# DLRM tower on one core: two-operand one-hot compares, paired lookups, gathers in eights

## The reference

```python
e = stack([tbl_f[ids[:, f]] for f in range(26)], axis=1)      # 2048 x 26 x 128
combined = concatenate([e, r_dense_x[:, None, :]], axis=1)    # 2048 x 27 x 128
z = einsum('bfd,bgd->bfg', combined, combined)[:, TRIU_I, TRIU_J]   # 351 pairs
h = concatenate([z, r_dense_x], axis=1)                       # 2048 x 479
h = maximum(h @ W_top1 + b_top1, 0)                           # 512
h = maximum(h @ W_top2 + b_top2, 0)                           # 256
y = h @ W_top3                                                # 2048 x 1
```

## Time and profile before

| | |
|---|---|
| Time, median of 3 runs | 373.29 us (373.04 to 374.13) |
| Profiled execution | 374.87 us |
| Its span, first to last instruction | 373.1 us |
| TensorE matmuls busy | 339.7 us (91%) |
| Weight loads busy | 312.7 us (84%) |
| VectorE busy | 194.0 us (52%) |
| ScalarE busy | 184.3 us (49%) |
| GpSimd busy | 254.9 us (68%) |
| Mean granted TensorE clock | 0.995 of full speed |

### The profile page before, as it was taken

The page is one execution under the profiler, slowest core; times in us unless marked ns, Lnnn a source line. Parts: engine busy times, 40 slices in busy tenths (PEclk is TensorE's granted clock), DMA queues, the critical chain, the costliest instruction groups (busy, mean ns, idle before and its releaser), DMA issues.

```text
span 373.1 us, 13958 instructions
## 1 busy us (share of the span) xinstructions
PE 339.7 (91%) x6176; PEld 312.7 (84%) x6176; DVE 194.0 (52%) x700; ACT 184.3 (49%) x234; POOL 254.9 (68%) x265
## 2 busy tenths in 40 slices
PE   0775879599999999999999999999999999999986
PEld 0775879598989988999989989999888988998776
DVE  1998758274645734575645634575545635541020
ACT  3783711673337463573437552582526552574332
POOL 6877777777777777777777777776777677771000
PEclk9998999999999999999999999999999999999999
DMA  7974761221532216222432126221442122210000
GB/s 266 368 244 157 223 215 53 52 66 53 177 87 67 57 52 208 57 66 52 145 115 72 51 54 206 51 72 47 121 142 67 46 59 66 53 50 26 16 2 4
DMA packets 15777, 37.17 MB, mean 100 GB/s; under 512 B 5125, under 2 KB 7813, under 8 KB 15716
## 3 DMA queue, kind: packets, MB, share of 16 engines
q0 software_dynamic: 8192, 16.79, 16.8%
q1 hardware_dynamic: 7524, 19.48, 15.5%
HBM read 36.24 MB, written 0.01 MB: 97 GB/s over the span
## 4 chain that ended last, share of the span: by engine, by line
PE 86%; POOL 5%; issue 4%; ACT 3%; DMA 3%; ACTq 0%
PE ps_lk L442 38%; PE ps_gram L469 14%; PE ps_tr L454 8%; PE ps_mlp L499 8%; PE ps_zt L499 7%; POOL rows L218 5%; PE ps_mlp L508 4%; PE ps_zt L508 4%; DMA rows<-in_tbl,gather_ids 2%; PE ps_mlp L516 2%; PE ps_zt L486 2%; ACT xt L319 1%; ACT xt L309 1%; DMA gather_ids<-in_ids_gather 1%; ACT ids_from L304 0%
## 5 line engine op out<-in xcount | busy, mean ns | idle before, releaser
L218 POOL DMA_INDIRECT rows<-in_tbl,gather_ids x256 | 253.5, 990 | 82.3 <-issue 70.7
L252 DVE TENSOR_SCALAR onehot<-ids_from 128x256 fp32r<-128x256 f32 x640 | 151.7, 303 | 59.3 <-PE ps_lk L442 42.6
L442 PE MATMUL ps_lk<-onehot,table 128*128 128x256 f32 x1280 | 166.9, 289 | 13.2 <-DVE onehot L252 11.5
L442 PEld LDWEIGHTS ps_lk<-onehot,table 128*128 128x128 f32 x1280 | 159.1, 195 | 13.9 <-issue 12.4
L319 ACT COPY xt<-ps_tr 128x512 f32<-128x512 f32 x64 | 76.6, 1197 | 96.5 <-PE ps_tr L454 94.6
L260 DVE STREAM_TRANSPOSE zs<-ps_gram 128x832 f32<-128x832 f32 x16 | 16.8, 1050 | 91.9 <-PE ps_gram L469 91.9
L469 PEld LDWEIGHTS ps_gram<-xt 128*26 128x26 f32 x4096 | 43.5, 103 | 19.5 <-issue 16.0
L469 PE MATMUL ps_gram<-xt 128*26 128x26 f32 x4096 | 52.2, 192 | 5.5 <-issue 1.3
L309 ACT COPY xt<-ps_lk 128x512 f32<-128x512 f32 x40 | 48.6, 1226 | 13.4 <-PE ps_lk L442 7.9
L454 PE MATMUL ps_tr<-ident,rows 128*128 128x128 f32 x256 | 39.9, 278 | 9.2 <-ACT xt L319 4.5
L454 PEld LDWEIGHTS ps_tr<-ident,rows 128*128 128x128 f32 x256 | 29.8, 141 | 13.2 <-issue 5.3
(11 more groups left out here) (30 smaller groups left out, 102.4 us busy)
## 6 DMA issues: line engine op xcount, KB each, us to landing
ids<-in_ids_onehot SPq DMA_DIRECT2D x16, 640.0 KB, 5.2
rows<-in_tbl,gather_ids POOLq DMA_INDIRECT x256
w<-in_tbl SPq DMA_DIRECT2D x6, 512.0 KB, 5.8
h<-in_tbl SPq DMA_DIRECT2D x2, 512.0 KB, 5.9
zt<-in_tbl SPq DMA_DIRECT2D x2, 512.0 KB, 5.7
dense_x<-in_dense SPq DMA_DIRECT2D x8, 128.0 KB
zt<-in_dense SPq DMA_DIRECT2D x8, 128.0 KB, 2.4
w<-in_w SPq DMA_DIRECT2D x1, 512.0 KB
```

What stands on the lines that cost most here:

```text
L218: pool.indirect_dma_start(rows[n % ROW_BUFS][:, r, :], None, t_[f"tbl_{GATHERED[r]}"], bass.IndirectOffsetOnAxis(ap=gather_ids[:, n, r:r + ...
L252: nc.vector.tensor_scalar(onehot[:, u % RING, :], ids_from[:, j, :], float(k), None, ALU.is_equal).then_inc(s_unit, 1)
L442: m = nc.tensor.matmul(bank(c, i)[:, j % 2, :], table[:, j, part, k, :], onehot[:, u % RING, :], start=(k == 0 and part == 0), stop=(k == ...
```

## The change

The one-hot rows. A unit is now one k for both tables of a lookup (512 columns), so a chunk has 40 units and the ring holds 8. In chunk 0 one compare with a number makes a unit, after both tables' subtractions. In chunks 1 to 7 (`make_pairs`) one two-operand compare makes two units (1024 elements): the ids of two tables, repeated for two k, against `row`, a small tile with the numbers 0 to 7 in each partition, two of them repeated along the samples. POOL and VectorE make `row` at the start.

The lookups. Both tables of a lookup are done side by side: for each k, table a high and low, table b high and low. The number and the shape of the matmuls stay. The ids are loaded and shifted in parts of 4 and 6 tables instead of 5 and 5.

The gathers. They are issued in eights (half a tile). The wait for the turn of the group is gone; a half waits for a count of used units (LEAD, the first two tiles and one half) or of grams.

The order. In chunk 0 each lookup is followed by one turn, and the third tile's turns move into chunk 1's loop. `layer2(c - 1, 1)` and `gram(c, 1, 1)` of the last chunk come before its `turn_pairs`. The last MLP runs layer by layer over both tiles, with banks of its own from those that the lookups no longer need, and both halves of y are copied at once.

```diff
-RING = 16
-UNITS = NO * KT
+RING = 8
+UNITS = LP * KT
+USE = 2
+CUT = (0, 4, NO)
+LEAD = (0, 2, 6, 10, 16)
+LAST = (CHUNKS - 1) * MLP_USES
...
-        onehot = sb("onehot", [P, RING, CS], F32R)
+        onehot = sb("onehot", [P, RING, 2, CS], F32R)
+        row = sb("row", [P, KT])
...
+        def last1_bank(t, j):
+            return ps_lk[j][:, 0, 0:P] if j < LB else (ps_tr, ps_mlp)[t][:, 0:P]
+        def last2_bank(t, j):
+            return ((ps_tr, ps_zt)[j][:, 0:P], ps_lk[j][:, 0, 0:P])[t]
+        def last3_bank():
+            return ps_lk[2][:, 0, :]
...
         @block.gpsimd
             def gather(n, g):
-                if n >= ROW_BUFS:
-                    pool.wait_ge(s_tr, (n - ROW_BUFS) * NGR + g + 1)
-                    pool.sem_inc(s_carrier["pool"], 1)
                 for r in GROUPS[g]:
...
-            for n in range(ROW_BUFS):
-                for g in range(NGR):
-                    gather(n, g)
-            for n in range(ROW_BUFS, TILES):
+            for n in range(TILES):
                 for h in range(2):
-                    pool.wait_ge(s_gpart, (n - 2) * PARTS + h + 1)
+                    b = n * PARTS + h
+                    if 0 < b < len(LEAD):
+                        pool.wait_ge(s_unit_used, LEAD[b])
+                    elif b >= len(LEAD):
+                        pool.wait_ge(s_gpart, max(b - 2 * PARTS, 0) + 1)
                     gather(n, 2 * h)
                     gather(n, 2 * h + 1)
...
         @block.vector
-                    nc.vector.tensor_scalar(onehot[:, u % RING, :], ids_from[:, j, :],
+                    nc.vector.tensor_scalar(onehot[:, u % RING, :, :], ids_from[:, 2 * i:2 * i + 2, :],
                                             float(k), None, ALU.is_equal).then_inc(s_unit, 1)
+            def make_pairs(c, lo, hi):
+                for u in range(lo, hi, USE):
+                    i, k = divmod(u, KT)
+                    if k == 0 and 2 * i in CUT:
+                        dve.wait_ge(s_from, c * 2 + (CUT.index(2 * i) + 1))
+                    dve.wait_ge(s_unit_used, (c * UNITS + u - RING) // USE + 1)
+                    nc.vector.tensor_tensor(
+                        onehot[:, u % RING:u % RING + USE, :, :].rearrange("p u a s -> p u (a s)"),
+                        ids_from[:, 2 * i:2 * i + 2, :].rearrange("p a s -> p (a s)").unsqueeze(1).to_broadcast([P, USE, 2 * CS]),
+                        row[:, k:k + USE].unsqueeze(2).to_broadcast([P, USE, 2 * CS]), ALU.is_equal
+                    ).then_inc(s_unit, USE)
...
-                make_units(0, j * KT, (j + 1) * KT)
-            make_units(1, 0, 2 * PU)
+                if j % 2 == 1:
+                    make_units(0, (j - 1) // 2 * KT, (j + 1) // 2 * KT)
+            make_pairs(1, 0, 2 * KT)
...
         @block.tensor
-                for j in (2 * i, 2 * i + 1):
+                for k in range(KT):
+                    u = i * KT + k
                     if c == 0:
-                        pe.wait_ge(s_low, j + 1)
-                    for k in range(KT):
-                        u = j * KT + k
-                        if k % 2 == 0:
-                            pe.wait_ge(s_unit, c * UNITS + u + 2)
+                        pe.wait_ge(s_unit, u + 1)
+                    elif k % (KT // 2) == 0:
+                        pe.wait_ge(s_unit, c * UNITS + u + KT // 2)
+                    for j in range(2):
                         for part in range(2):
-                            m = nc.tensor.matmul(bank(c, i)[:, j % 2, :], table[:, j, part, k, :],
-                                                 onehot[:, u % RING, :],
+                            m = nc.tensor.matmul(bank(c, i)[:, j, :], table[:, 2 * i + j, part, k, :],
+                                                 onehot[:, u % RING, j, :], start=(k == 0 and j == 0 and part == 0),
...
-            lookup(0, 0)
-            turn(0, 0, 0)
-            lookup(0, 1)
-            turn(0, 0, 1)
-            turn(0, 0, 2)
-            lookup(0, 2)
-            turn(0, 0, 3)
-            lookup(0, 3)
-            turn(0, 1, 0)
-            lookup(0, 4)
-            turn(0, 1, 1)
+            for i in range(LP):
+                lookup(0, i)
+                turn(0, i // NGR, i % NGR)
             gram(0, 0, 0)
             lookup(1, 0)
             gram(0, 0, 1)
+            turn(0, 1, 1)
+            lookup(1, 1)
             turn(0, 1, 2)
-            lookup(1, 1)
+            lookup(1, 2)
             turn(0, 1, 3)
-            lookup(1, 2)
             gram(0, 1, 0)
-            turn(1, 0, 0)
-            turn(1, 0, 1)
-            turn(1, 0, 2)
             gram(0, 1, 1)
...
             c = CHUNKS - 1
             turn_pairs(c, 0)
-            layer2(c - 1, 1)
-            gram(c, 1, 1)
             layer3(c - 1)
+            last1(0, 0)
+            last1(0, 1)
+            turn_pairs(c, 1)
+            last1(0, 2)
+            last1(0, 3)
             for j in range(T1):
-                layer1(c, j, 0, P, c * CT + 1)
-            turn_pairs(c, 1)
-            for j in range(T2):
-                layer2(c, j, 0, P)
-            layer3(c, 0, P)
-            for j in range(T1):
-                layer1(c + 1, j, P, P, c * CT + 2)
-            for j in range(T2):
-                layer2(c + 1, j, P, P)
-            layer3(c + 1, P, P)
+                last1(1, j)
+            for t in range(CT):
+                for j in range(T2):
+                    last2(t, j)
+            last3()
```

More of the change, by code:

```diff
@@ L83, in build @@
         dense_x = sb("dense_x", [P, CS])
-        ids = [sb(f"ids{h}", [P, HALF, CS], I32) for h in range(2)]
+        ids = [sb(f"ids{h}", [P, CUT[h + 1] - CUT[h], CS], I32) for h in range(2)]
         ids_from = sb("ids_from", [P, NO, CS])
-        onehot = sb("onehot", [P, RING, CS], F32R)
+        onehot = sb("onehot", [P, RING, 2, CS], F32R)
         table = sb("table", [P, NO, 2, KT, D], F32R)
@@ L477, in turn_pairs @@
                     pe.wait_ge(s_zt, c * CT + t)
[L478 to L482, removed]
+                elif c > 0:
                     pe.wait_ge(s_act, (c - 1) * MLP_USES + T1 + T2)
@@ L498, in layer1, with layer2 @@
                     r = ZT[k][1] if k < NZ else D
-                    i = nc.tensor.matmul(mlp_bank(j)[:, 0:n], w1[0:r, k, j * P:(j + 1) * P], zt[0:r, k, lo:lo + n],
+                    i = nc.tensor.matmul(mlp_bank(j)[:, 0:CS], w1[0:r, k, j * P:(j + 1) * P], zt[0:r, k, :],
                                          start=(k == 0), stop=(k == NZ))
                 i.then_inc(s_mlp, 1)
-            def layer2(m, j, lo=0, n=CS):
+            def layer2(m, j):
                 pe.wait_ge(s_act, m * MLP_USES + T1)
-                if j == 1 and CHUNKS - 2 <= m < CHUNKS:
-                    pe.wait_ge(s_zt, CHUNKS * CT - (CHUNKS - 1 - m))
@@ L507, in layer2, with layer3 @@
                 for k in range(T1):
-                    i = nc.tensor.matmul(mlp_bank(T1 + j)[:, 0:n], w2[:, k, j * P:(j + 1) * P], h1[:, k, lo:lo + n],
+                    i = nc.tensor.matmul(mlp_bank(T1 + j)[:, 0:CS], w2[:, k, j * P:(j + 1) * P], h1[:, k, :],
                                          start=(k == 0), stop=(k == T1 - 1))
                 i.then_inc(s_mlp, 1)
-            def layer3(m, lo=0, n=CS):
+            def layer3(m):
                 pe.wait_ge(s_act, m * MLP_USES + T1 + T2)
-                for t in range(n // P):
+                for t in range(CT):
@@ L515, in layer3, with last1 @@
                     for k in range(T2):
-                        i = nc.tensor.matmul(mlp_bank(T1 + T2)[:, t:t + 1], h2[:, k, lo + t * P:lo + (t + 1) * P],
+                        i = nc.tensor.matmul(mlp_bank(T1 + T2)[:, t:t + 1], h2[:, k, t * P:(t + 1) * P],
+                                             cols[:, T1 + T2 + k:T1 + T2 + k + 1], start=(k == 0), stop=(k == T2 - 1))
+                i.then_inc(s_mlp, 1)
+            def last1(t, j):
+                if j == 0:
+                    pe.wait_ge(s_zt, (CHUNKS - 1) * CT + t + 1)
+                    pe.wait_ge(s_densez, CHUNKS * 16)
+                if t > 0:
+                    pe.wait_ge(s_act, LAST + min(j, LB - 1) + 1)
+                for k in range(NZ + 1):
+                    r = ZT[k][1] if k < NZ else D
+                    i = nc.tensor.matmul(last1_bank(t, j), w1[0:r, k, j * P:(j + 1) * P], zt[0:r, k, t * P:(t + 1) * P],
+                                         start=(k == 0), stop=(k == NZ))
+                i.then_inc(s_mlp, 1)
@@ new lines, in last2, with last3 @@
+            def last2(t, j):
+                pe.wait_ge(s_act, LAST + (t + 1) * T1)
+                for k in range(T1):
+                    i = nc.tensor.matmul(last2_bank(t, j), w2[:, k, j * P:(j + 1) * P], h1[:, k, t * P:(t + 1) * P],
+                                         start=(k == 0), stop=(k == T1 - 1))
+                i.then_inc(s_mlp, 1)
+            def last3():
+                for t in range(CT):
+                    pe.wait_ge(s_act, LAST + CT * T1 + (t + 1) * T2)
```

(36 more changed lines are left out.)

153 lines of the change are left out of this document (82 added, 71 removed).

## The result

| | before | after |
|---|---|---|
| Time, median | 373.71 us (4 runs) | 413.81 us (4 runs, 410.89 to 415.46) |
| Ratio | | 1.105 (95% interval 1.100 to 1.110) |
| Span of the profiled execution | 373.1 us | 411.6 us |
| POOL busy | 254.9 us | 303.5 us |
| Last gather starts at | 336.99 us | 383.72 us |

The forecast was 414 us, slower. The page of the changed kernel, with the lines that answer to the earlier trace rows: POOL, 5% of the chain before, now holds 63% of it.

The account below looks back on a forecast made before the run. POOL, a second bound hidden behind TensorE, was to become the bound: last rows at 389.8 us, plus 22.9 tail and 1.2 clock, 413.9 us of span, plus 0.2: 414 us, own range 402 to 430 (wider range 366 to 432).

Parts of the forecast that it names:

- The compare on POOL: Chunks 1 to 7: two-input compares make POOL's gathers wait, 8.5 us per chunk, 60 us in all.
- The second hit in a run: Within a run of four compares, the second wait of a POOL gather costs 1.02 us.
- The first hit of the runs of four: In a run of four compares without a gap, the first wait of a POOL gather costs 0.57 us.
- the runs of eight: Lookups 3 and 4 adjacent give eight compares in a row, once per chunk, costing POOL 3.6 us.
- The phase: Gathers under compares: POOL returns 1.25 us after a boundary, misses the next at 1.14, waits for 2.28.
- Rival 2: Compares 1.25 us or more apart: gathers hit every boundary, POOL loses 16 us, span 369 to 370; chance 0.10.
- POOL's end: POOL's gathers, ended at 337.9 us before, would end at 387 to 388 us.
- The tail: From the last turn of rows to the end: 22.9 us instead of 27.1, from the reordered MLP.
- The surcharge for the clock: At the end, 1.2 us added because TensorE's granted clock falls after waits for the last turns.
- The front: Chunk 0 and early lookups: 7 to 8 us sooner on TensorE, worth nothing with POOL as bound.
- rival 1: The two-input compare with broadcast operands leaves POOL alone, TensorE stays the bound: 361.5 us, faster; chance 0.12.
- TensorE's clock: TensorE waits several us for each last turn; after such waits its clock fell before (0.91 mean); 1.2 us added.

Follow-up runs that it names:

- e1: The changed kernel with the one-input compare (512 elements, one unit each) back in chunks 1 to 7, all else changed: 373.53 us, ratio 0.996.
- e2: The kernel before with one edit, a two-input compare of 1024 elements for four one-input ones in chunks 1 to 7: 410.57 us, ratio 1.096.
- e5: The changed kernel, but chunk 1's compares read the row of numbers from PSUM: 404.61 us, ratio 1.080 to the kernel before (second run).
- e3: The changed kernel with a VectorE memset of 128 elements behind each two-input compare: 379.66 us, ratio 1.013 to the kernel before.
- e4: The changed kernel with a VectorE memset of one element behind each two-input compare: 412.14 us, ratio 1.100 to the kernel before.
- e6: The changed kernel with two-input compares of half the size (512 elements, one unit each): 373.05 us, ratio 0.998 to the kernel before (second run).
- e8: The kernel before with only the change's new end (last chunk's order, last MLP layer by layer): 370.64 us, ratio 0.991 (second run).
- e7: The changed kernel with one-input compares of 256 elements and no waits for used units: 368.59 us, ratio 0.985 to the kernel before (second run).

## Why the prediction was right

**The compare on POOL** (forecast 60 us, bounds 0 to 71): 54.9 us. The step is shown by e1 and e2, which take it away and do it alone, and by e5, which names its cause. The size was 5 us too large: 0.39 us per compare, not 0.43. The second hit in a run was met to 0.01 us: 1.01 to 1.03 us in every run of three or more, where 1.02 was forecast. The first hit of the runs of four was 0.50 us on average, not 0.57. And the runs of eight, forecast once per chunk at 3.6 us, stood whole only in chunk 1 (3.5 us); the other compares came in 26 runs of four, five of three, two of two and nine alone. Two readings behind this term were off as well, by little: a gather among one-input compares waited up to 0.12 us, not 0.08 at most, and a compare hit at random costs 0.52 us by its own rows (1.14 x 1.14 / 2 / 1.25), not 0.46, so the upper bound is 73 us, not 71.

**The phase** (misses 1.14, waits for 2.28): right, and more narrowly than I wrote. The boundary is missed at 1.13 and 1.15 and hit at 1.22, not from 1.25 on (e3, e4, e6). Rival 2 was thus nearer than its chance of 0.10 says: 0.08 us more per compare made most of it true (e3).

**POOL's end** (387 to 388): 384.7. Less for the compares, and 1.6 us more for the first count of used units, which I had called harmless: POOL stood before it until 16.2 us, when the first half of lookup 0 was done. That step of the sum failed, hidden by the other.

**The tail** (22.9 + 1.2): 25.2 us from the turn at 386.40. The sum of the reordered work was right, by e8 to 0.1 us (the terms as listed add up to 22.7, not 22.9). The surcharge for the clock was wrong: the granted clock was 1.00 from 380 us to the end. TensorE had two holes inside the two last grams, 1.76 us and 0.51, put down to its own issue; e8 has none of them there, and what makes them the runs don't tell.

**The front** (7 to 8 us on TensorE, worth nothing): worth nothing in the changed kernel, right. The first gram came at 41.66, not 39 (39.06 in e1), since the turn ahead of it waited 3.66 us for rows. But rival 1's 361.5 us took all 7.6 us as gain, and so did e1's expectation. In e7 all of it is worth 5.6 us, of which the tail is 3.3 (e8), so some 2 us are left for the front. A lead of TensorE is worth only what POOL can follow: e1 waited 3.0 us for rows and had lost it by 125 us, e7 waited for none.

**TensorE's clock**: 0.959 on average in this kernel, whose TensorE waits 32.2 us for rows. Slices of 20 us have a mean of 0.83 or 0.91, a part of each at 1.2 GHz instead of 2.4; the lookups' matmuls are busy 174.0 us instead of 166.9. It did not lengthen the tail, and ahead of that TensorE waits for POOL anyway.

**Why the time was met to 0.2 us**: partly luck. The span is 411.6 us where 413.9 were forecast: 3.1 less for POOL's end, 0.3 less from there to the last turn, 1.1 more for the tail. The median of the runs lies 2.2 us above the profiled span. The forecast added 0.2, and that step was wrong: it set the median (373.29) against the span of a slower execution (374.87 with a span of 373.1). Each execution took 1.7 to 2.0 us longer than its own span, here 413.38 with a span of 411.6. Two errors of some 2 us, one each way, gave the 0.2.

## What to carry to other kernels

An engine at 68% busy can be a bound: take its first and last instruction and the gaps between, not its share. A two-input VectorE instruction from SBUF stops GpSimd's gathers until it ends, and what it costs hangs on its length against the gather's 1.25 us: compares 0.60 us apart cost nothing against the kernel before (e6), 1.22 us apart with a gap between them 5 us (e3), 1.13 us apart 40 us. Long VectorE instructions beside gathers should have one SBUF input, be short, or read the second from PSUM.

## What the runs showed of the hardware

Adding 140 memsets that take 0.08 us each between two compares made a kernel 34 us faster (e3 against the changed one), as two engines fell out of a bad phase. A gather that asks 0.05 to 0.08 us after a two-input compare has begun is let in and the compare waits (0.72 to 0.75 us instead of 0.68, e6); at 0.10 us it waits for the whole compare (e4). With the second input in PSUM a compare of the same size and length holds no gather: 0.94 us under it instead of 1.97 (e5). One-input compares hold gathers a little, those of 512 elements more (at most 0.25 us, 15.0 us in all, e1) than twice as many of 256 (at most 0.13, 11.8 us in all, e7), with less time on VectorE (141.7 us of compares against 194.0).
